# Cross-attention on one core: maxima taken over two heads at a time, masked keys replaced by a mean

## The chip, the core and the metric

The kernel runs on one NeuronCore of a Trainium2 chip. The metric is device time in microseconds: the median of several executions of the whole program, launch to end. A profile is one execution under the hardware profiler, with a time of its own. TensorE does the matrix products, VectorE, ScalarE and GpSimd (POOL in the rows) the elementwise work, and the queue SP issues nearly all DMAs.

## The reference

One cross-attention block in float32: batch B = 4, 512 query tokens, 512 key tokens, width 512, 16 heads of 32, MLP width 2048.

```python
x = layer_norm(hidden_states, ln1_w, ln1_b)
q = x @ q_w + q_b;  k = enc @ k_w + k_b;  v = enc @ v_w + v_b      # split into 16 heads of 32
scores = einsum('bhqd,bhkd->bhqk', q, k) / sqrt(32)
scores = where(mask, scores, finfo.min)                            # mask: (B, keys)
out = einsum('bhqk,bhkd->bhqd', softmax(scores), v) @ cproj_w + cproj_b
hidden = out + hidden_states
y = gelu(layer_norm(hidden, ln2_w, ln2_b) @ fc_w + fc_b) @ proj_w + proj_b
return hidden + y
```

## The kernel before, in words

**Precision.** Every product is made of three float32r matmuls: each operand is split into a high part (its float32r rounding) and a low part (the rest), and high times high, low times high and high times low are summed in PSUM (`mm3`, L487 to L489). So each product tile needs a rounding and a subtraction by ScalarE, VectorE or GpSimd.

**Stage 1, projections** (batch b = 0 to 3). For each batch TensorE computes V (4 units), K (4 units g = 0 to 3) and Q (4 units). Each unit is 12 matmuls. ScalarE writes a unit's high part (`qk_high`, L778), VectorE its low part (`qk_low`, L994), into one of four buffers `QK`; SP stores both to DRAM (`store_qk`, L269). A buffer is written again four units later and waits for both stores. On VectorE the LN1 statistics and norms of the next batch (`x_norm`, L930 to L943) and the affine step (`x_affine`, L986) lie between these. `x_turn(1)` (L547), TensorE's transposes of batch 1, comes after batch 0's last Q unit and before batch 1's V, and waits for all four norms of `x_norm(1)`. GpSimd makes the low parts of weights, context and x (`low`, L1224), in a fixed order.

**Stage 2, attention.** Sets s = 0 to 15: set s holds the four heads j = 0 to 3 of batch s // 4, group s % 4. Softmax needs a maximum per head and query. It is taken over *leading scores*: the product of the high parts alone. `s1(group)` (L579) computes, for one set and one block of 128 queries, the four heads' 128x512 tiles into the four PSUM banks 0 to 3, in one go; `maximum(tile)` (L1007) reads one bank, adds the mask row (0 or a huge negative number, spread over 128 partitions in SBUF by `load_mask`) and takes the maximum into one column of `mx`. There are 64 groups and 256 tiles. Groups 0 to 7 lie between the last batch's projections; the loop of 64 passes `i` (s = i // 4, kc = i % 4) does group 8 + i in pass i, for i up to 55. One ring (`RB`) orders everything that uses banks 0 to 3; `s1` waits until all earlier places are evicted.

In a pass TensorE runs, in program order: the exact transposed scores of key block kc (`s2`, L594, four tiles, three PSUM banks in turn; the mask is a row of the stacked operand), `s1` of the group ahead, P times V of pass i - 2 (`pv`, L610), at kc = 0 the transpose of the maxima (L586), at kc = 2 the sums of the previous set (`sums`, L625), and in some odd passes from i = 17 on (and 56 to 59) a *piece* of the output projection (`cproj`, six matmuls) into a bank of the same ring. `s1` of the next pass stands behind all that. ScalarE takes the exponentials (`exp`, L796). VectorE takes the group's maxima, then the divide steps of an older set (`divide_a`, L1012, at kc = 2 once the sums are there; L1016; L1022 at kc = 0), then adds the piece to the residual (L1134), later the pair adds of probabilities (L1036, which GpSimd does before pass 56, L1324), and for batch 0 the LN2 statistics (passes 36 to 44), the block transposes `y_block` (passes 48, 49, 52, 53) and the affine steps `y_affine` (L962, all four in pass 56). The transposed blocks of LN2 go out to DRAM (`y_store`) and come back (`y_load`, issued at pass 54); `y_affine` waits for their landing. ScalarE and GpSimd then split them (`Y_HIGH`, `Y_LOW`: passes 57 to 59).

**Stage 3, MLP.** 64 passes of `fc` and `pj`, nearly all TensorE.

Each engine executes its own program in order; a wait at the head of a queue holds everything behind it.

## Time and profile before

| | us |
|---|---|
| median of 3 executions | 779.47 (778.07 to 779.97) |
| the profiled execution | 775.62 |
| its span | 773.8 |
| TensorE busy | 745.1 (96%) |
| VectorE busy | 461.9 (60%) |
| ScalarE busy | 281.4 (36%) |
| GpSimd busy | 292.9 (38%) |
| the 256 masked maxima, rows' own time | 169.0 (84.5 + 84.5) |
| chain that ended last: TensorE, VectorE | 77%, 15% of the span |

Busy time counts overlapping rows once. Stage 1 ends and the attention loop begins at about 152 us from the start of the span, the loop ends at about 408 us. In a timeline row the first two numbers are the start and the length in us, then come engine, line, operation, output <- input, the shapes and a count; the bracket gives how long the engine stood idle before it and what released it.

### The profile page before, as it was taken

To read this page: it belongs to the slowest core of one execution; us is meant where nothing else is said; L and a number is where in the kernel's file an instruction comes from. 1 tells how busy PE (TensorE), PEld (TensorE's weight loads), DVE (VectorE), ACT (ScalarE), POOL (GpSimd) and SP (SyncE) were. 2 spreads that over 40 slices of the span, in tenths; PEclk is the share of its full clock that TensorE was granted. 3 is DMA by queue.
4 is the path that set the end of the run, shared out by engine and by line. 5 is a ranking of instruction groups with operands and counts; after the bars stand their busy time and mean duration, and the time that the engine had idled before them with its cause. 6 is when DMAs were issued, how large, how long until landed. Compare 5 with 4: busy or idle time off the path is not lost.

```text
span 773.8 us, 10036 instructions
## 1 busy us (share of the span) xinstructions
PE 745.1 (96%) x3664; PEld 515.3 (67%) x3664; DVE 461.9 (60%) x999; ACT 281.4 (36%) x492; POOL 292.9 (38%) x179
## 2 busy tenths in 40 slices
PE   6999999889899999999989999999999999999998
PEld 5878886633344444444436888888888888888886
DVE  6673346789988888999768578534413343232213
ACT  4434241276766666666763011211112111211110
POOL 2654150067898778799734002122002200230000
PEclk9999999999999999999999999999999999999999
DMA  9656377597656785578640637240220404030001
GB/s 327 227 169 226 126 212 245 186 253 167 171 141 153 189 217 150 156 204 181 173 136 28 191 102 211 82 163 1 42 68 1 163 14 97 1 108 1 1 0 55
DMA packets 94385, 103.25 MB, mean 133 GB/s; under 512 B 39968, under 2 KB 48420, under 8 KB 94336
## 3 DMA queue, kind: packets, MB, share of 16 engines
q1 hardware_dynamic: 94192, 102.59, 46.1%
q8 instruction: 29, 0.48, 0.3%
q14 instruction: 20, 0.16, 0.1%
q10 hardware_dynamic: 144, 0.02, 0.0%
HBM read 73.08 MB, written 29.37 MB: 132 GB/s over the span
## 4 chain that ended last, share of the span: by engine, by line
PE 77%; DVE 15%; DMA 2%; issue 2%; ACT 2%; SPq 1%; POOL 0%; DVEq 0%; ACTq 0%
PE ps L487 21%; PE ps L489 21%; PE ps L488 21%; DVE ps L1007 8%; PE ps L610 4%; PE ps L594 4%; PE ps L579 3%; PE ps L625 2%; DVE R L1134 2%; DMA yt<-FU 1%; DVE mx L1007 1%; PE ps L547 1%; ACT Pt L796 1%; DVE R L943 1%; DVE V L1036 1%
## 5 line engine op out<-in xcount | busy, mean ns | idle before, releaser
L796 ACT ACTIVATE Pt<-ps 128x512 f32<-128x512 f32 x256 | 137.6, 597 | 75.0 <-PE ps L594 74.2
L1181 DVE CAST HR<-R 128x512 fp32r<-128x512 f32 x52 | 25.1, 483 | 184.7 <-ACT R L831 184.7
L831 ACT ACTIVATE R<-ps,cols 128x512 f32<-128x512 f32 x52 | 35.9, 690 | 227.2 <-PE ps L489 227.1
L594 PE MATMUL ps<-BIG 98*128 98x512 f32 x256 | 92.9, 440 | 6.5 <-ACT Pt L796 2.6
L1007 DVE CUSTOM_DVE_ANT_0 ps<-ps,FU 128x512 f32<-128x512 f32 x128 | 84.5, 722 | 14.4 <-PE ps L579 14.2
L594 PEld LDWEIGHTS ps<-BIG 98*128 98x128 f32 x256 | 44.6, 189 | 70.3 <-issue 29.2
L1007 DVE CUSTOM_DVE_ANT_0 ps<-ps,BIG 128x512 f32<-128x512 f32 x128 | 84.5, 723 | 8.4 <-PE ps L579 8.4
L487 PE MATMUL ps<-BIG,HR 128*128 128x512 f32 x192 | 74.8, 390 | 0.7 <-DVE HR L1183 0.7
L487 PE MATMUL ps<-YT,BIG 128*128 128x512 f32 x192 | 74.9, 390 | 0.0
L488 PE MATMUL ps<-YT,BIG 128*128 128x512 f32 x192 | 74.7, 389 | 0.0
L489 PE MATMUL ps<-BIG,HR 128*128 128x512 f32 x192 | 74.7, 389 | 0.0
L489 PE MATMUL ps<-YT,BIG 128*128 128x512 f32 x192 | 74.7, 389 | 0.0
L488 PE MATMUL ps<-BIG,HR 128*128 128x512 f32 x192 | 74.7, 389 | 0.0
L610 PE MATMUL ps<-Pt,V 128*32 128x512 f32 x512 | 68.2, 605 | 0.0
L1324 POOL TENSOR_TENSOR R<-Pt 128x1024 f32<-128x1024 f32 x20 | 47.8, 2409 | 49.0 <-ACT Pt L796 49.0
L487 PE MATMUL ps<-BIG 128*128 128x512 f32 x128 | 53.1, 415 | 5.9 <-DVE BIG L1075 5.9
L1224 POOL TENSOR_TENSOR YT<-R,YT 128x512 fp32r<-128x512 f32 x12 | 15.4, 1308 | 109.1 <-ACT YT L848 109.1
L1324 POOL TENSOR_TENSOR RAWY<-Pt 128x1024 f32<-128x1024 f32 x22 | 52.9, 2426 | 4.0 <-ACT Pt L796 4.0
L1224 POOL TENSOR_TENSOR BIG<-R,BIG 128x512 fp32r<-128x512 f32 (+1 forms) x27 | 36.7, 1377 | 42.6 <-ACT BIG L808 23.0
L488 PE MATMUL ps<-BIG 128*128 128x512 f32 x128 | 51.5, 402 | 0.0
L489 PE MATMUL ps<-BIG 128*128 128x512 f32 x128 | 51.4, 401 | 0.0
L487 PE MATMUL ps<-BIG,WK 128*128 128x512 f32 x128 | 50.8, 397 | 0.0
(133 smaller groups left out, 1375.3 us busy)
## 6 DMA issues: line engine op xcount, KB each, us to landing
BIG<-qs SPq DMA_DIRECT2D x62, 256.0 KB, 2.9
BIG<-ks SPq DMA_DIRECT2D x62, 256.0 KB, 3.2
ks<-BIG SPq DMA_DIRECT2D x32, 256.0 KB, 2.1
qs<-BIG SPq DMA_DIRECT2D x32, 256.0 KB, 5.2
R<-hd SPq DMA_DIRECT2D x28, 256.0 KB, 4.1
R<-in_x SPq DMA_DIRECT2D x16, 256.0 KB, 5.9
hd<-R SPq DMA_DIRECT2D x16, 256.0 KB, 3.9
yt<-FU SPq DMA_DIRECT2D x64, 64.0 KB, 2.1
```

The lines of the kernel that those rows point to most:

```text
L487: eng.matmul(outp, a[0], b[0], start=first, stop=False)
L488: eng.matmul(outp, a[1], b[0], start=False, stop=False)
L489: return eng.matmul(outp, a[0], b[1], start=False, stop=last)
L579: eng.matmul(bank(bank_b(RB[("s1", 4 * group + j)])), lead(s)[r, 0, qc * 128:(qc + 1) * 128], lead(s)[r, 1, :], start=True, stop=True).the ...
L594: eng.matmul(bk, K_[0:98, j, kc * 128:(kc + 1) * 128], Q_[0:98, j, :], start=True, stop=True).then_inc(S["p_ra"], 1)
L610: ins = eng.matmul(bank(7)[32 * j:32 * j + 32, :], V[:, 4 * b + kc, c:c + 32], Pt[:, r, j % 2, :], start=kc == 0, stop=kc == 3)
L796: eng.activation(Pt[:, r, j % 2, :], bank(bank_a(("s2", i, j))), ACT.Exp, scale=SCALE).then_inc(S["a_ra"], 1)
L831: eng.activation(g, bank(4 + i % 2), ACT.Gelu_apprx_tanh, bias=fcb[:, f:f + 1]).then_inc(S["a_g"], 1)
L1007: eng.tensor_tensor_reduce(out=scores, in0=scores, in1=MASK[s // 4], scale=1.0, scalar=-3.4e38, op0=ALU.add, op1=ALU.max, accum_out=mx[:, ...
L1181: eng.tensor_copy(HR[:, n, 0, :], g).then_inc(S["v_hh"], 1)
L1224: eng.tensor_tensor(dst, src, high.bitcast(F32), ALU.subtract).then_inc(S[name], 1)
L1324: eng.tensor_tensor(pair(m)[:, 2 * hp:2 * hp + 2, :], Pt[:, (r - 2) % 6, :, :], Pt[:, r, :, :], ALU.add).then_inc(S["g_ac"], 1)
```

## The change

1. The maxima are no longer taken tile by tile with the mask. `maxima(n)` takes two heads (two PSUM banks, 1024 elements per partition) in one `tensor_reduce` that writes two columns of `mx`: 128 instructions for 256. `s1` signals after every second matmul, and the ring has two places per group for four. The mask rows in SBUF, their four loads and the semaphores go away.
2. So that masked keys can't win a maximum, their columns in the leading part of K are replaced by the mean of the kept keys' columns. `keys(b)` (six small and middle VectorE instructions per batch) makes two rows, `kept` and `share`, from the mask's bytes, which one new DMA spreads over the partitions early; `keep` (a multiply with a running sum, then a multiply-add) rewrites one 128x512 tile. For batches 0 to 2 that is `keep_key`, straight after each K unit's `qk_low`, and the store of the high part waits for it. For batch 3 it is `keep_lead(s)`, on the loaded leading part, in passes 38, 42, 46 and 50. `keys(3)` is in pass 0.
3. The negated maxima get a bias for rows with no kept key, in the same ScalarE instruction.
4. The projection pieces have fixed banks, 0 or 2. A piece waits for the first pair of the current group to be evicted.
5. The `y_affine` steps move from pass 56 to 58, `Y_HIGH` to 59 and 60, `Y_LOW` to 60 and 61.
6. The load of `cbt` moves from stage 1 to pass 2, behind a wait for `keys(3)`'s first step.

```diff
-        MASK = [FU[:, 0, :], FU[:, 1, :], BIG[:, 2048:2560].bitcast(F32), BIG[:, 2560:3072].bitcast(F32)]
+        bits = cbt[:, :].bitcast(U8)
+        def kept(b):
+            return FU[:, 0, :] if b < B - 1 else BF[:, 2048:2560]
+        def share(b):
+            return FU[:, 1, :] if b < B - 1 else BF[:, 2560:3072]
...
-        Y_NORM, Y_BLOCKS, Y_AFFINE = (45, 47, 49, 51), (48, 49, 52, 53), (56, 56, 56, 56)
-        Y_HIGH, Y_LOW = (57, 57, 58, 58), (58, 58, 59, 59)
+        Y_NORM, Y_BLOCKS, Y_AFFINE = (45, 47, 49, 51), (48, 49, 52, 53), (58, 58, 58, 58)
+        Y_HIGH, Y_LOW = (59, 59, 60, 60), (60, 60, 61, 61)
...
-        def bank_b(place):
-            return place % 4
+        def bank_cp(i):
+            return 2 if i in (56, 58) else 0
...
# SP
-                for h, done in ((0, ("a_qh", kq + 1)), ...
+                for h, done in ((0, ("a_qh", kq + 1) if which or b == B - 1 else ("v_kf", 4 * b + g + 1)), ...
-            def load_mask(b):
...
+            eng.dma_start(bits, mask.rearrange("b t -> (b t)").partition_broadcast(128)).then_inc(S["d_bits"], 16)
...
                 if i == 2:
-                    load_mask(1)
-                if i in (12, 28):
-                    load_mask(2 if i == 12 else 3)
+                    sp.wait_ge("v_mc", 4)
+                    eng.dma_start(cbt[:, :], c_b.partition_broadcast(128)).then_inc(S["d_cb"], 16)
...
# TensorE
             def s1(group):
                 s, qc = divmod(group, 4)
                 pe.wait_ge(f"d_hi{s % 2}", 32 * (s // 2 + 1))
-                ring_b(RB[("s1", 4 * group + 3)])
+                if s >= 4 * (B - 1):
+                    pe.wait_ge("v_kf", s + 1)
+                place = RB[("s1", 2 * group)]
+                if place:
+                    pe.wait_ge("v_rb", place)
+                else:
+                    pe.wait_ge("v_fu", 16)
                 for j in range(4):
                     r = slice(32 * j, 32 * j + 32)
-                    eng.matmul(bank(bank_b(...)), lead(s)[r, 0, ...], lead(s)[r, 1, :], start=True, stop=True).then_inc(S["p_rb"], 1)
+                    ins = eng.matmul(bank(j), lead(s)[r, 0, ...], lead(s)[r, 1, :], start=True, stop=True)
+                    if j % 2:
+                        ins.then_inc(S["p_rb"], 1)
...
                 if i in PIECES:
                     n, c, half = PIECES[i]
-                    bk = ring_b(RB[("cp", n, c, half)])
-                    cproj(n, c, (2 * half, 2 * half + 1), bk).then_inc(S["p_rb"], 1)
+                    if i in GROUPS:
+                        pe.wait_ge("v_rb", RB[("s1", 2 * GROUPS[i])] + 1)
+                    else:
+                        pe.wait_ge("v_rb", RB[("cp", n, c, half)] - 1)
+                    cproj(n, c, (2 * half, 2 * half + 1), bank(bank_cp(i))).then_inc(S["p_rb"], 1)
...
# VectorE
-            def maximum(tile):
...
-                eng.tensor_tensor_reduce(out=scores, in0=scores, in1=MASK[s // 4], scale=1.0, scalar=-3.4e38, op0=ALU.add,
-                                         op1=ALU.max, accum_out=mx[:, s % 2, 4 * j + qc:4 * j + qc + 1]).then_inc(S["v_rb"], 1)
+            def keys(b):
+                dve.wait_ge("d_bits", 16)
+                if b == B - 1:
+                    dve.wait_ge("p_pj", 40)
+                eng.tensor_copy(kept(b), bits[:, 512 * b:512 * b + 512]).then_inc(S["v_mc"], 1)
+                dve.wait_ge("v_mc", b + 1)
+                eng.tensor_reduce(out=cnt[:, b:b + 1], in_=kept(b), op=ALU.add, axis=AX.X).then_inc(S["v_ct"], 1)
+                dve.wait_ge("v_ct", b + 1)
+                eng.tensor_scalar(rn[:, b:b + 1], cnt[:, b:b + 1], 1.0, -1.0, ALU.max, ALU.mult).then_inc(S["v_cm"], 1)
+                eng.tensor_scalar(nz[:, b:b + 1], cnt[:, b:b + 1], 0.0, 2.0 ** 127, ALU.is_equal, ALU.mult).then_inc(S["v_nz"], 1)
+                dve.wait_ge("v_cm", b + 1)
+                eng.reciprocal(rn[:, b:b + 1], rn[:, b:b + 1]).then_inc(S["v_rn"], 1)
+                dve.wait_ge("v_rn", b + 1)
+                eng.tensor_scalar(share(b), kept(b), 1.0, rn[:, b:b + 1], ALU.subtract, ALU.mult).then_inc(S["v_sh3"], 1)
+            def keep(s, part):
+                b = s // 4
+                dve.wait_ge("v_sh3", b + 1)
+                eng.tensor_tensor_reduce(out=part, in0=part.bitcast(F32), in1=kept(b), scale=1.0, scalar=0.0, op0=ALU.mult,
+                                         op1=ALU.add, accum_out=ksum[:, s % 4:s % 4 + 1]).then_inc(S["v_ks"], 1)
+                dve.wait_ge("v_ks", s + 1)
+                eng.scalar_tensor_tensor(out=part, in0=share(b), scalar=ksum[:, s % 4:s % 4 + 1], in1=part.bitcast(F32),
+                                         op0=ALU.mult, op1=ALU.add).then_inc(S["v_kf"], 1)
+            def keep_key(b, g):
+                dve.wait_ge("v_ql", 8 * b + g + 1)
+                keep(4 * b + g, QK[(8 * b + g) % 4][:, 0, :])
+            def keep_lead(s):
+                dve.wait_ge(f"d_hi{s % 2}", 32 * (s // 2 + 1))
+                keep(s, lead(s)[:, 1, :])
+            def maxima(n):
+                group, h = divmod(n, 2)
+                s, qc = divmod(group, 4)
+                dve.wait_ge("p_rb", RB[("s1", n)] + 1)
+                if s >= 2:
+                    dve.wait_ge("p_ra", RA[("mt", s - 2)] + 1)
+                eng.tensor_reduce(out=mx[:, s % 2, 8 * h + qc:8 * h + qc + 5:4], in_=ps[h][:, :, :], op=ALU.max,
+                                  axis=AX.X).then_inc(S["v_rb"], 1)
...
+            keys(0)
             dve.wait_ge("d_raw00", 32)
             eng.tensor_copy(WKQ[2][:, 0:2, :], raw[0][:, 0:2, :]).then_inc(S["v_hi"], 1)
             for b in range(B):
...
                 if 0 < b < 3:
                     x_norm(b + 1)
+                    keys(b)
                 for g in range(4):
                     if b == 0 and g == 2:
                         x_affine(0)
                     qk_low(b, g, 0)
+                    if b < 3:
+                        keep_key(b, g)
...
+                if i == 0:
+                    keys(B - 1)
                 if kc == 2 and s >= 1:
                     divide_a(s - 1)
...
+                if kc == 2 and 4 * (B - 1) <= s + 3 < NS:
+                    keep_lead(s + 3)
```

## Rows read from the trace of the kernel before

**Rows 1.** The stretches by engine (us busy of each, granted clock, DMA), three of them.
```profile
60.00:100.00 40.00, 40.00 (x186) 33.35 (x185) 15.23 (x28) 13.40 (x21) 10.80 (x7) 1.00 0.51 184
...
160.00:200.00 40.00, 35.90 (x216) 12.56 (x212) 36.12 (x98) 28.17 (x56) 30.41 (x15) 1.00 0.73 171
...
386.00:393.00 7.00, 4.37 (x18) 2.99 (x11) 4.25 (x5) 3.93 (x9) 7.00 (x5) 0.78 0.34 117
```

**Rows 2.** VectorE's groups, shapes apart: the masked maxima, and a small one.
```profile
L1007 DVE CUSTOM_DVE_ANT_0 ps<-ps,FU 128x512 f32<-128x512 f32 x128 | 84.5, 722 | 14.4 <-PE ps L579 14.2
...
L939 DVE TENSOR_SCALAR ve<-mv 128x4 f32<-128x4 f32 x8 | 1.4, 170 | 0.3
```

**Rows 3.** Timeline of the leading scores on TensorE, passes 13 and 14.
```profile
199.39 0.51 PE L579 MATMUL ps<-BIG 32*128 32x512 f32 x4 [0.35 <-DVE mx L1007]
...
202.68 0.51 PE L579 MATMUL ps<-BIG 32*128 32x512 f32 x4 [0.46 <-DVE mx L1007]
```

**Rows 4.** Timeline of the same, passes 40 to 42, and VectorE at 40.
```profile
308.37 0.51 PE L579 MATMUL ps<-BIG 32*128 32x512 f32 x4 [0.17 <-DVE R L1134]
...
308.87 0.70 DVE L1007 CUSTOM_DVE_ANT_0 ps<-ps,BIG 128x512 f32<-128x512 f32 x1 [0.48 <-PE ps L579]
...
311.62 0.50 PE L579 MATMUL ps<-BIG 32*128 32x512 f32 x4 [0.33 <-DVE mx L1007]
...
315.98 0.51 PE L579 MATMUL ps<-BIG 32*128 32x512 f32 x4
```

**Rows 5.** Timeline of VectorE and TensorE in the first batch's projections.
```profile
21.73 0.68 DVE L1088 CAST WK<-RAWY 128x1024 fp32r<-128x1024 f32 x1
...
26.30 2.96 DVE L986 TENSOR_SCALAR R<-ps,cols 128x512 f32<-128x512 f32 x4
...
33.27 0.39 PE L487 MATMUL ps<-BIG,WK 128*128 128x512 f32 x1
...
33.51 2.46 DVE L930 BATCH_NORM_STATS2 st<-R 128x6 f32<-128x512 f32 x4
...
37.59 6.06 DVE L943 TENSOR_SCALAR R<-R,mv,rs 128x512 f32<-128x512 f32 x4 [1.13 <-POOL rs L1229]
...
43.70 1.97 PE L547 MATMUL ps<-ident,R 128*128 128x128 f32 x16 [0.74 <-DVE R L943]
```

**Rows 6.** Timeline of GpSimd in the same stretch.
```profile
22.49 4.75 POOL L1224 TENSOR_TENSOR WK<-RAWY,WK 128x1024 fp32r<-128x1024 f32 x2 [3.41 <-DVE WK L1088]
...
27.85 5.04 POOL L1224 TENSOR_TENSOR BIG<-R,BIG 128x512 fp32r<-128x512 f32 x4 [0.62 <-ACT BIG L762]
...
37.52 4.92 POOL L1224 TENSOR_TENSOR BIG<-RAWY,BIG 128x1024 fp32r<-128x1024 f32 x2
```

**Rows 7.** Timeline: one subtraction of two SBUF tiles on VectorE, alone and beside GpSimd.
```profile
178.16 0.64 DVE L1145 TENSOR_TENSOR BIG<-R,BIG 128x512 fp32r<-128x512 f32 x1
...
201.82 5.16 POOL L1324 TENSOR_TENSOR R<-Pt 128x1024 f32<-128x1024 f32 x2
...
202.48 2.26 DVE L1145 TENSOR_TENSOR BIG<-R,BIG 128x512 fp32r<-128x512 f32 x1
```

**Rows 8.** Timeline around pass 39: the divide's transpose, TensorE's projection piece, GpSimd.
```profile
303.41 0.72 DVE L1012 STREAM_TRANSPOSE R<-ps 128x512 f32<-128x512 f32 x1 [0.48 <-PE ps L625]
...
305.94 0.39 PE L487 MATMUL ps<-BIG 128*128 128x512 f32 x1
...
306.24 1.30 POOL L1224 TENSOR_TENSOR BIG<-BF,BIG 128x512 fp32r<-128x512 f32 x1 [3.06 <-ACT BIG L808]
```

**Rows 9.** Timeline of passes 57 to 59: the affine step, the transpose, TensorE.
```profile
378.77 2.66 DVE L962 TENSOR_SCALAR HN<-HN,cols 128x512 f32<-128x512 f32 x2 [1.96 <-DMA HN<-yt]
...
381.82 2.32 DVE L962 TENSOR_SCALAR HN<-HN,cols 128x512 f32<-128x512 f32 x2 [0.39 <-DMA HN<-yt]
...
388.52 0.70 DVE L1012 STREAM_TRANSPOSE R<-ps 128x512 f32<-128x512 f32 x1
...
389.27 0.72 PE L594 MATMUL ps<-BIG 98*128 98x512 f32 x2 [2.63 <-DVE R L1012]
```

More of the change, by code:

```diff
@@ L62, in cross_attention_block @@
         mT = sb("mT", [16, 128], R)
+        kk = sb("kk", [128, 16], F32)
+        cnt, rn, nz, ksum = [kk[:, 4 * i:4 * i + 4] for i in range(4)]
         def part(base, off, k):
@@ L180, in plan_rings @@
         def plan_rings():
-            a, b, seats = {("mt", 0): 0}, {("s1", n): n for n in range(4 * EARLY)}, [("mt", 0)]
+            a, b, seats = {("mt", 0): 0}, {("s1", n): n for n in range(2 * EARLY)}, [("mt", 0)]
             for i in range(NI):
@@ L194, in plan_rings @@
                 if i in GROUPS:
-                    for j in range(4):
-                        b[("s1", 4 * GROUPS[i] + j)] = len(b)
+                    for h in range(2):
+                        b[("s1", 2 * GROUPS[i] + h)] = len(b)
                 if i in PIECES:
@@ L266, in store_qk @@
                 scr = (ks, qs)[which]
-                for h, done in ((0, ("a_qh", kq + 1)), (1, ("v_ql", kq + 1) if (b, g, which) != (*LAST_Q, 1) else ("g_ql", 1))):
+                for h, done in ((0, ("a_qh", kq + 1) if which or b == B - 1 else ("v_kf", 4 * b + g + 1)), (1, ("v_ql", kq + 1) if (b, g, which) != (*LAST_Q, 1) else ("g_ql", 1))):
                     sp.wait_ge(*done)
@@ L562, in ring_a @@
                 return bank(bank_a(item))
-            def ring_b(place):
-                if place >= 4:
-                    pe.wait_ge("v_rb", place - 3)
-                else:
-                    pe.wait_ge("v_fu", 13 + place)
-                return bank(bank_b(place))
             def s1(group):
@@ L1090, in _ @@
                 if b == 3:
-                    for j in range(12):
-                        maximum(j)
+                    for n in range(6):
+                        maxima(n)
                 if 0 < b < 3:
                     x_norm(b + 1)
+                    keys(b)
                 for g in range(4):
@@ L1098, in _ @@
                     qk_low(b, g, 0)
+                    if b < 3:
+                        keep_key(b, g)
                     if b == 3 and g in EARLY_K:
-                        for j in range(4):
-                            maximum(4 * EARLY_K[g] + j)
+                        for h in range(2):
+                            maxima(2 * EARLY_K[g] + h)
                 if b == 0:
@@ L1111, in _ @@
                     if b == 3 and g in EARLY_Q:
-                        for j in range(4):
-                            maximum(4 * EARLY_Q[g] + j)
+                        for h in range(2):
+                            maxima(2 * EARLY_Q[g] + h)
             for i in range(NI):
@@ L1119, in _ @@
                 if i in GROUPS:
-                    for m in range(4):
-                        maximum(4 * GROUPS[i] + m)
+                    for h in range(2):
+                        maxima(2 * GROUPS[i] + h)
+                if i == 0:
+                    keys(B - 1)
                 if kc == 2 and s >= 1:
@@ L1133, in _ @@
                         dve.wait_ge("g_xc", 4 * n + c + 1)
-                    eng.tensor_tensor(R2[:, c, :], bank(bank_b(place)), R2[:, c, :], ALU.add).then_inc(S["v_rb"], 1)
+                    eng.tensor_tensor(R2[:, c, :], bank(bank_cp(i)), R2[:, c, :], ALU.add).then_inc(S["v_rb"], 1)
                 if kc == 3 and s >= 1:
```

34 lines of the change are left out of this document (10 added, 24 removed).

## The prediction

> **What bounds the kernel now.** I read the stretches by engine first: they say which engine sets the pace of each stage, which the totals of the whole span can't. In stage 1 TensorE is without a gap (40.00 of 40 us) while VectorE has 25 us to spare; in the attention loop both are nearly full (35.90 and 36.12) [rows 1]. So a VectorE microsecond is worth something only in the loop, and a TensorE stall in stage 1 is lost for good.
>
> Next the masked maxima: 256 of them, a row of 0.722 us each [rows 2], and the question is which passes wait for them. The timeline of `s1` answers it. Early in the loop an `s1` stands idle on VectorE's `mx` (0.35 and 0.46) and passes are 3.29 long [rows 3]: 0.5 of matmuls, then the group's maxima, then the next `s1`. From pass 16 on a block of four passes takes 16.3 us, and in only one of the four does `s1` wait for maxima: in 40 to 41 (3.25 us, idle 0.33). The `s1` of pass 42 shows no wait, and that of 40 waits 0.17 for the residual add L1134, behind the projection piece, not for maxima [rows 4]. So most of the time VectorE loses on maxima is hidden there.
>
> Last, the timeline of two places that the change touches. In batch 0, `x_turn(1)` waits 0.74 us for VectorE's norms L943: here VectorE's order of work bounds TensorE [rows 5]. And around pass 57, `y_affine` blocks VectorE from 376.8 (378.77 less its idle 1.96) to 384.14, so that the transpose L1012 comes at 388.52 and TensorE stands for 2.63 us [rows 9]; in the 7 us around it the granted clock is 0.78, part of the time at 1.2 in place of 2.4 GHz [rows 1].
>
> **The maxima.** Removed: four instructions per group. On VectorE the group takes 2.70 us from the first start to the release (308.87 to 311.57, 0.05 ahead of `s1` at 311.62 [rows 4]). The trace has no `tensor_reduce`. The nearest row is the statistics instruction, which also reads 512 elements per partition and writes little: four in 2.46, so one starts each 0.60 [rows 5]. Of that 0.53 is a rate of one element per cycle as 512-wide rows have it (0.60 less 0.07 fixed), so 1024 elements take about 1.13 start to start and 1.23 as a row; a pair ends after 1.13 + 1.23 = 2.36, 0.3 sooner than now. The bounds: 2.80 if two banks cost as two rows of 0.70 [rows 4] in sequence (0.1 later than now), and 2.27 if the last row's tail overlaps too. I take 2.36, as the statistics row is of the same kind. The Trainium skill (VectorE: DVE Perf Modes, the TRN2 errata section) charges 120 cycles plus one per element for a PSUM source at 0.96 GHz, an estimate of 1.19 us each and 2.38 a pair; this would change each saving by hundredths.
>
> What it is worth, by place. Between the last projections two `s1` wait for maxima in the timeline: 2 x 0.3 = **-0.6**. In passes 1 to 15 ten intervals hang on VectorE; seven give their full 0.3 (2.1), three others 0.8 together, because other work comes up first; `keys(3)` in pass 0 pushes the next maxima by 0.6, of which 0.2 reaches `s1`: **-2.7**. From pass 16 ten blocks give 0.3 each, -3.1, as TensorE's own work then ends at the same time. In four of them VectorE has statistics or a `y_block` (0.6 to 0.7) ahead of the second pass's maxima, and the piece there now waits for a pair (1.2) where it waited for a single tile (0.7): 4 x 0.45 = 1.8 lost. Together **-1.3**.
>
> **keep_lead.** Four times, in passes 38, 42, 46, 50, two instructions of 512 elements. The nearest row is the subtraction L1145, two SBUF inputs, 0.64 alone [rows 7]; with the reading of the accumulator and a wait between, 1.4 for the two. VectorE's queue puts them behind L1012, which in pass 38 ends at 304.13 [rows 8]; GpSimd is idle then, until 306.24. Queued behind them are the maxima of the next pass, which began 0.3 after L1012; they come 1.1 late, and the piece, which started at 305.94 [rows 8], waits for the first pair until 306.85. That pass is one of those bound by the piece and L1134, so 0.9 is lost each time: **+3.6**. It would be nothing if the pass had slack; its idle of 0.17 on L1134 [rows 4] excludes that.
>
> **keys and keep_key, batches 1 and 2.** Three instructions of 0.6 and three of 0.17 [rows 2, 5], 2.3 us per `keys`, and 1.4 to 3.5 per `keep_key`. VectorE's 25 idle us in 40 cover them [rows 1]; without that cover it would be 8 us a batch. The later stores of K delay no buffer, as it is rewritten four units later (11 us). I take 0. The spread of the mask's bytes (256 KB) is out 15 us ahead of its use; the four mask loads that go away hid behind other work: 0.
>
> **keys(0) and keep_key(0, g).** Here the cover is thin, and this is the largest term. I walk VectorE's queue. `keys(0)` stands before L1088, which moves from 21.73 to 23.95 [rows 5]. GpSimd's two lows of q_w, 2.4 each, follow it and move from 22.49 to 24.7 [rows 5, 6]. The question is whether the two-input `keep` instructions are held by GpSimd. The row of before that is of this kind says so: L1145 takes 0.64 alone and 2.26 when GpSimd's pair add is under way, and it ends 0.6 after that pair add does [rows 7]. The four norms do the same: 6.06 for four, two of them waiting out GpSimd's 4.92 [rows 5, 6]. So: `qk_low` 0 ends at 25.3; the first instruction of `keep` waits for GpSimd until 27.1, the second for the other low until 30.1 and ends at 30.75; `qk_low` 1 and an unheld `keep` end at 32.85. `x_affine(0)` starts there instead of at 26.30. GpSimd's four lows of x follow 1.55 behind (27.85 before [rows 6]), so from 34.4; `keep` 2 is held twice and pushes the last low to 40.7; `keep` 3 ends at 42.1. The statistics of batch 1 start at 42.1 instead of 33.51, and the norms and `x_turn(1)` come 8.6 later. TensorE meanwhile waits for the lows of x: Q's first unit, second half, moves from 33.27 [rows 5] to 40.7, so it reaches `x_turn(1)` at 50.4 and still waits until 52.3. Loss **+8.6**. The other bound is the same walk with nothing held: 2.2 for keys, 5.6 for four `keep`, less the idle gaps in between: the statistics start at 36.0, **+2.5**. I take 8.6, by rows 7.
>
> The Trainium skill (SBUF — State Buffer, Who interferes with whom) has the rule: a VectorE instruction with two SBUF inputs contends with a GpSimd instruction that reads SBUF. The trace agrees (0.64 against 2.26); that a multiply with a running sum falls under it no row of before shows. By the rule the term is 8.6, without it 2.5.
>
> **y_affine to pass 58.** VectorE then runs the pair adds of pass 57 at once, L1012 comes at about 383.6 when the sums are there, and TensorE's 2.63 us go, and with them 7.0 x 0.22 = 1.5 of clock: -4.1. The data land at 381.8, before VectorE gets to pass 58 (385.9), so the wait goes and isn't moved. Given back: ScalarE's two-by-two roundings (1.1 each pair) now lie in passes 59 and 60, where exponentials set the pace: +1.0. **-3.1**, bounds -4.1 and 0.
>
> **Sum.** 8.6 - 0.6 - 2.7 - 1.3 + 3.6 - 3.1 = +4.5. Against the profiled execution (775.62) that is 780.1. The median of the runs is 779.47, 3.85 above it, and I forecast what runs will show: 784.0. A measurement of this kernel tells about 0.3% (2.3 us) from no change.
>
> **Rivals.**
> *Slower still: the reduction over two banks is no shorter than two rows* (the fusion doesn't do what it says). Then a group takes 2.80 us, 0.44 more than I take, on some 22 waits, with the piece's wait longer too: +10, 794 at the worst, 790 with the tail gain. For: no row shows a reduce. Against: statistics start each 0.60. Chance 0.10.
> *Nothing is held and the tail gives all.* Place: batch 0, VectorE between 25 and 42. Price: 2.5 for 8.6, and -4.1 for -3.1: the sum is 4.5 - 6.1 - 1.0 = -2.6, **776.9, faster**. It decides from the point where the statistics of batch 1 start before about 36. For: L1007, with one input in PSUM, is not held beside GpSimd (its rows stay 0.70 to 0.73). Against: rows 7. Chance 0.17.
> *Held in part.* Only one of the two instructions of `keep` is held, or GpSimd falls in other gaps: +4 to 5 in batch 0, sum near 0, 779.5. For: the walk above hangs on who comes first by tenths. Chance 0.23.
> *The forecast.* 0.50.
>
> Slower by over 0.3%: forecast and first rival, 0.60; within: the third, 0.23; faster: 0.17. The range takes in the second rival's 776.9 and, above, the forecast with no tail gain (787) and part of the first rival: 777 to 789. The forecast's own range is 781 to 788.
>
> **What would show it.** `tensor_reduce` rows near 1.23, 128 of them, start to start 1.13; `s1` of pass 41 not waiting for VectorE. In batch 0: `keep` rows of 2 us and more beside GpSimd, the statistics of batch 1 at 42, `x_turn(1)` near 52, TensorE idle some 8 us between 32 and 52. The two `keep_lead` rows at 0.65 and pass 39 about 0.9 longer. No stall near pass 58, clock 1.00 there. Wrong, if `keep` rows stay at 0.65 in batch 0, if `x_turn(1)` starts before 47, or if the reduces take 1.4.

## The result, and the profile after

| us | before | after |
|---|---|---|
| median (20 executions each, same chip) | 778.88 | 781.48 |
| fastest, slowest | 772.72, 789.61 | 780.90, 790.94 |
| profiled execution, span | 775.62, 773.8 | 781.28, 779.5 |
| maxima, rows' own time | 169.0 in 256 | 150.6 in 128 |

The ratio after to before is 1.006 (95%: 1.0035 to 1.0086): slower, by less than the 784.0 forecast. The medians hide something: the fastest executions differ by 8.2 us, not by 2.6. 19 of the 20 of after lie between 780.9 and 784.0. Of before, 8 lie between 772.7 and 774.9 and 11 between 778.0 and 782.8. Those are not two clean groups: before was timed again beside the experiments, and there 21 of 94 executions fill the gap between (one of 1844 us is left aside). The experiments come back to this. Their ratios are against the executions of before taken beside each of them (medians 777.1 to 778.5).

The views answer to those of before. First the groups of VectorE's lines, and for the two instructions of `keep` on a K unit the forms with shortest, median and longest row.

```profile
L1044 DVE TENSOR_REDUCE mx<-ps 128x2 f32<-128x1024 f32 x128 | 150.6, 1219 | 22.0 <-PE ps L581 22.0
```

```profile
L1024 DVE CUSTOM_DVE_ANT_0 BIG<-BIG,FU x12: 691/693/2316, 25.4 to 112.1; 128x512 fp32r<-128x512 f32 x12
```

```profile
L1027 DVE SCALAR_TENSOR_TENSOR BIG<-FU,kk,BIG x12: 752/752/2767, 27.8 to 112.9; 128x512 fp32r<-128x512 f32 x12
```

A reduce takes 1.219 us for two tiles, where [rows 2] had 0.722 for each: 0.23 less. The `keep` instructions are 0.69 and 0.75 where nothing is in their way, and up to 2.32 and 2.77. (The 2.77 stands in batch 2, at 112.87, where it costs nothing.) What happens in batch 0, the timeline of VectorE there says (to be read against [rows 5]):

```profile
24.61 0.74 DVE L999 SCALAR_TENSOR_TENSOR BIG<-ps,cols,BIG 128x512 fp32r<-128x512 f32 x1
25.39 2.32 DVE L1024 CUSTOM_DVE_ANT_0 BIG<-BIG,FU 128x512 fp32r<-128x512 f32 x1
...
27.75 2.75 DVE L1027 SCALAR_TENSOR_TENSOR BIG<-FU,kk,BIG 128x512 fp32r<-128x512 f32 x1
...
31.20 0.69 DVE L1024 CUSTOM_DVE_ANT_0 BIG<-BIG,FU 128x512 fp32r<-128x512 f32 x1
...
31.94 0.75 DVE L1027 SCALAR_TENSOR_TENSOR BIG<-FU,kk,BIG 128x512 fp32r<-128x512 f32 x1
32.61 2.96 DVE L991 TENSOR_SCALAR R<-ps,cols 128x512 f32<-128x512 f32 x4
...
37.63 0.81 DVE L1024 CUSTOM_DVE_ANT_0 BIG<-BIG,FU 128x512 fp32r<-128x512 f32 x1
...
38.48 1.65 DVE L1027 SCALAR_TENSOR_TENSOR BIG<-FU,kk,BIG 128x512 fp32r<-128x512 f32 x1
...
42.23 2.47 DVE L938 BATCH_NORM_STATS2 st<-R 128x6 f32<-128x512 f32 x4
```

GpSimd's rows and TensorE's waits in the same stretch:

```profile
24.77 5.18 POOL L1269 TENSOR_TENSOR WK<-RAWY,WK 128x1024 fp32r<-128x1024 f32 x2 [5.37 <-DVE WK L1126]
34.15 5.42 POOL L1269 TENSOR_TENSOR BIG<-R,BIG 128x512 fp32r<-128x512 f32 x4 [4.20 <-ACT BIG L768]
```

```profile
36.91 0.77 PE L490 MATMUL ps<-BIG,WK 128*128 128x512 f32 x1 [3.99 <-POOL BIG L1269]
52.41 0.77 PE L550 MATMUL ps<-ident,R 128*128 128x128 f32 x5 [1.55 <-DVE R L951]
```

The first `keep` waits out GpSimd's two lows of q_w, one with each of its instructions. The chain of delays is that of the forecast: `x_affine(0)` 6.3 later than in [rows 5], GpSimd's lows of x at 34.15, statistics of batch 1 at 42.23 for 33.51, `x_turn(1)` at 52.41 for 43.70. Busy time by stretch, with TensorE's granted clock ahead of the DMA share, shows the clock down behind TensorE's idle 3.99 us, part of the time at 1.2 GHz:

```profile
35.00:40.00 5.00, 3.09 (x7) 2.12 (x8) 3.66 (x5) 4.19 (x6) 4.58 (x4) 0.58 0.01 3
40.00:45.00 5.00, 5.00 (x17) 4.00 (x17) 4.90 (x13) 0.69 (x1) 0.00 (x0) 0.74 0.65 216
```

To place the rest I took the start of each `s1` group from the timelines and subtracted that of the profile before. Group 8 is pass 0, group 24 pass 16, group 63 pass 55; `pv` is its last pair of matmul rows. Positive is later. The kernels of the experiments are in the same table.

| profile of | group 0 | 8 | 22 | 26 | 44 | 63 | last `pv` |
|---|---|---|---|---|---|---|---|
| before, start us | 119.91 | 151.82 | 202.68 | 218.59 | 292.12 | 368.91 | 406.00 |
| after | +8.72 | +8.01 | +5.96 | +5.69 | +4.46 | +8.53 | +5.26 |
| e1 | 0.14 | 0.15 | -0.18 | 9.09 | 9.11 | 9.04 | 5.78 |
| e2 | 3.82 | 3.10 | 2.07 | 9.16 | 7.96 | 11.99 | 8.73 |
| e3 | 0.69 | -0.07 | -2.29 | -2.56 | -3.79 | 0.25 | -3.02 |
| e4 | 1.82 | 4.31 | 3.34 | 3.07 | 1.89 | 4.97 | 1.70 |
| e5 | 0.27 | 0.28 | 0.49 | 0.21 | 0.25 | 0.25 | -2.06 |
| e6 | 1.42 | 0.71 | -0.33 | -0.60 | -1.77 | 0.58 | -2.69 |
| e7 | 1.00 | 0.29 | -1.65 | -1.91 | -3.12 | -2.66 | -5.94 |
| e8 | 9.00 | 8.53 | 7.51 | 13.99 | 13.43 | 18.64 | 15.38 |
| e9 | 0.39 | 0.40 | -0.08 | 4.34 | 4.38 | 4.40 | 2.10 |
| e10 | 0.15 | 0.11 | 1.33 | 6.10 | 6.07 | 6.05 | 4.06 |
| e11 | 9.32 | 8.59 | 7.65 | 7.41 | 6.16 | 10.19 | 7.88 |
| e12 | 3.07 | 3.94 | 2.94 | 2.71 | 1.55 | 2.02 | -1.24 |

So after loses 8.7 us ahead of the first `s1`, all in batch 0, wins back 3 by pass 18 and another 1.2 by pass 36, loses 4.1 from there to pass 55, and wins 3.3 in the tail.

### The profile page after: what moved, and what is told of

It reads as the page before. It is cut to its first block, busy times and chain, and to the rows that moved or that the text cites. A ratio compares the mean times of both kernels' runs of the same rounds, so it can differ in the third digit from the quotient of the medians.

```text
span 779.5 us, 9725 instructions
## 1 busy us (share of the span) xinstructions
PE 749.3 (96%) x3664; PEld 515.8 (66%) x3664; DVE 480.6 (62%) x687; ACT 281.0 (36%) x492; POOL 297.6 (38%) x179
## 4 chain that ended last, share of the span: by engine, by line
PE 77%; DVE 16%; issue 3%; ACT 2%; DMA 1%; SPq 0%; POOL 0%; DVEq 0%; ACTq 0%; POOLq 0%
PE ps L490 21%; PE ps L492 20%; PE ps L491 20%; DVE mx L1044 6%; PE ps L613 5%; PE ps L597 5%; PE ps L581 3%; PE ps L628 3%; DVE R L1177 2%; DVE R L951 1%; ACT Pt L804 1%; DVE BIG L1188 1%; DMA R<-in_k_w 1%; DVE BIG L1024 1%; PE ps L550 1%
## 5 line engine op out<-in xcount | busy, mean ns | idle before, releaser
L1044 DVE TENSOR_REDUCE mx<-ps 128x2 f32<-128x1024 f32 x128 | 150.6, 1219 | 22.0 <-PE ps L581 22.0
L490 PE MATMUL ps<-BIG,WK 128*128 128x512 f32 x128 | 52.2, 408 | 4.0 <-POOL BIG L1269 4.0
L492 PE MATMUL ps<-BIG,WK 128*128 128x512 f32 x128 | 50.9, 397 | 0.0
```

The source lines that it names most:

```text
L490: eng.matmul(outp, a[0], b[0], start=first, stop=False)
L492: return eng.matmul(outp, a[0], b[1], start=False, stop=last)
L1044: eng.tensor_reduce(out=mx[:, s % 2, 8 * h + qc:8 * h + qc + 5:4], in_=ps[h][:, :, :], op=ALU.max, axis=AX.X).then_inc(S["v_rb"], 1)
```

## The experiments

**e1: before with part 5 alone.** What is the tail gain, without the rest?

```diff
-        Y_AFFINE = ..., (56, 56, 56, 56); Y_HIGH, Y_LOW = (57, 57, 58, 58), (58, 58, 59, 59)
+        Y_AFFINE = ..., (58, 58, 58, 58); Y_HIGH, Y_LOW = (59, 59, 60, 60), (60, 60, 61, 61)
```

> The kernel before with part 5 alone: y_affine in pass 58, the roundings behind it in 59 and 60. My theory: VectorE no longer blocks in pass 56, so TensorE's idle 2.6 us near pass 59 and the lower clock behind it go, and about 1 us comes back in passes 59 and 60: 3.1 us less than the kernel before in its profiled execution (775.6), so about 772.5, ratio 0.996. Rival A (the wait only moves to pass 58): no change, and VectorE idle in front of y_affine there. Rival B (the stall also makes the spread of the runs of before, 772 to 782 us): then these runs lie close together, below all or nearly all of those of before.

Measured: 778.36 (772.58 to 781.79), ratio 1.0004 (0.9969 to 1.0039). In the profile the tail does give 3.3 (9.04 to 5.78), but the median and the fastest execution don't show it. Rival B fell as well, since the runs lie as far apart as those of before. And this profile lost 9.3 us between groups 22 and 26, in passes 14 to 17, where the edit changes nothing. VectorE, GpSimd, TensorE and the stretches there, in this order:

```profile
202.31 5.82 DVE L1145 TENSOR_TENSOR BIG<-R,BIG 128x512 fp32r<-128x512 f32 x1
```

```profile
201.65 4.69 POOL L1324 TENSOR_TENSOR R<-Pt 128x1024 f32<-128x1024 f32 x2
```

```profile
210.79 0.80 PE L579 MATMUL ps<-BIG 32*128 32x512 f32 x4 [3.98 <-DVE mx L1007]
```

```profile
205.00:210.00 5.00, 1.82 (x14) 0.43 (x6) 5.00 (x8) 2.32 (x4) 3.52 (x3) 0.90 1.06 226
210.00:215.00 5.00, 4.21 (x16) 1.46 (x16) 4.12 (x14) 0.78 (x2) 0.31 (x1) 0.50 0.20 75
215.00:220.00 5.00, 5.00 (x18) 1.58 (x18) 3.03 (x9) 2.59 (x6) 4.62 (x2) 0.50 0.02 5
220.00:225.00 5.00, 5.00 (x17) 1.72 (x17) 2.95 (x9) 2.46 (x5) 4.03 (x4) 0.50 0.93 243
225.00:230.00 5.00, 4.91 (x30) 2.63 (x33) 2.48 (x6) 2.40 (x5) 2.52 (x2) 0.90 1.06 225
```

The subtraction L1145 is the very row that [rows 7] show at 2.26 us, one pair add long, started 0.66 behind GpSimd's, as here. Here it lasts 5.82 and waits out both pair adds. In the profile of before GpSimd's two rows take 5.16, here 4.69. I read this as VectorE getting in between the two there and not here. TensorE then stands for 4 us and runs for 15 at 1.2 GHz. Neither price was in my sum, since the one profiled execution of before had been spared them.

**e2: after, with batch 0's `keep` made of two reductions with one input each** (what they write is not the mean: the replacement in batch 0 is left out). The count of instructions, their length and the waits stay; only the second SBUF input goes.

```diff
+                if b == 0:
+                    eng.tensor_reduce(out=ksum[...], in_=part.bitcast(F32), op=ALU.add, axis=AX.X).then_inc(S["v_ks"], 1)
+                    dve.wait_ge("v_ks", s + 1)
+                    eng.tensor_reduce(out=ksum[...], in_=part.bitcast(F32), op=ALU.add, axis=AX.X).then_inc(S["v_kf"], 1)
+                    return
                 eng.tensor_tensor_reduce(
```

> The changed kernel, but keep of batch 0 (four times) is two one-input sums of 512 elements in place of the two two-input instructions; the leading part of batch 0 is not rewritten (masked keys of batch 0 keep their values in the maxima). The same number of instructions, waits and elements. Theory (GpSimd holds two-input instructions): the sums stay at 0.69 us beside GpSimd, the statistics of batch 1 start at about 36 us instead of 42, x_turn(1) near 46 instead of 52.4; 781.3 - 6 = 775. Rival (the cost is the added work and its waits, not the hold): nothing moves, 781.

Measured: 778.11 (775.75 to 786.13), ratio 1.0018 (0.9976 to 1.0059). VectorE's timeline:

```profile
25.47 0.69 DVE L1025 TENSOR_REDUCE kk<-BIG 128x1 f32<-128x512 f32 x1
26.19 0.69 DVE L1027 TENSOR_REDUCE kk<-BIG 128x1 f32<-128x512 f32 x1
...
37.34 2.46 DVE L938 BATCH_NORM_STATS2 st<-R 128x6 f32<-128x512 f32 x4
```

Beside the same two GpSimd instructions no row is longer than 0.69. The statistics start at 37.34 for 42.23 and `x_turn(1)` at 47.51 for 52.41: 4.9 of the 8.7 us are the hold, 3.8 the bare queue time (I had bounded that at 2.5). The fastest execution falls by 5.2. This profile again has the long subtraction in pass 13 (6.18 us) and loses 7.1 between groups 22 and 26, so its total says nothing.

**e3: after without `keep_key` in batch 0** (masked keys of batch 0 are then not replaced).

```diff
-                    if b < 3:
+                    if 0 < b < 3:
                         keep_key(b, g)
```

> The changed kernel without keep_key in batch 0 (masked keys of batch 0 keep their values in the maxima); keys(0) stays. Theory: the statistics of batch 1 start near 33.8 again; keys(0) alone still moves GpSimd's lows of q_w and with them the lows of x by 1.6 us, of which x_turn(1)'s old wait of 0.7 hides a part: 0.5 to 1.2 us of the 8.7 stay, so 781.3 - 7.8 = 773.5. Rival (the loss comes from keys(0) or the mask's DMA at the start): 779 or more.

Measured: 774.45 (772.92 to 780.58), ratio 0.9962 (0.9924 to 1.0001). Group 0 is 8.0 earlier than in after, `x_turn(1)` at 44.18, and the fastest execution falls by 8.0. So four `keep_key` in one batch are 8.0 of the loss of 8.7; those of batches 1 and 2 cost nothing (the differences at `x_turn` 1, 2 and 3 are 8.71, 8.72 and 8.72), as forecast.

**e4: batch 0's replacement moved to the loaded leading parts at the end of stage 1**, where batch 3's is, `keys(0)` to batch 2 (the loads of the mask and of these leading parts move with them), and the `keep_lead` of batch 3 ahead of `divide_a`.

```diff
-            keys(0)
...
                 if b == 3:
+                    keep_lead(0)
+                    keep_lead(1)
                     for n in range(6):
                         maxima(n)
...
                     if b == 3 and g in EARLY_K:
                         for h in range(2):
                             maxima(2 * EARLY_K[g] + h)
+                    if b == 3 and g == 1:
+                        keep_lead(2)
...
+                    if b == 3 and g == 0:
+                        keep_lead(3)
                     if b == 3 and g in EARLY_Q:
```

> The changed kernel with the added work moved to idle places: batch 0's leading parts are rewritten after loading like batch 3's (sets 0 and 1 at the end of batch 2, 2 and 3 between the last projections), keys(0) in batch 2, its rows in a free part of RAWY, and keep_lead in passes 38 to 50 ahead of the divide's transpose. Theory: the 8.7 us of batch 0 go, the 3.7 of keep_lead shrink to at most 0.8, nothing new comes on the path: 781.3 - 8.7 - 3.2 = 769.4, ratio to before 0.988 to 0.992. Rival (the added VectorE work costs its length wherever it lies): the sum of it, 16 keeps of 1.45 and 4 keys of 2.2, stays, and the time is above 778.

Measured: 776.27 (774.22 to 780.77), ratio 0.9979 (0.9947 to 1.0011). Batch 0 is cured (`x_turn(1)` at 44.19), but the median is 6.9 us above the 769.4 expected. In the profile, 1.1 are lost at group 0, where VectorE waits for the landing of the leading part, and 4.1 between groups 6 and 9. The four `keep_lead` still cost 2.6 together (0.30, 0.05, 1.32 and 0.93 for their passes), where 0.8 was expected. There `keep_lead(3)` stands at 147.13 ahead of the maxima of group 6, TensorE waits 1.81 for them, and its granted clock is 0.72, 0.84 and 0.76 in the three stretches from 150 to 165. Not all of the 4.1 is the slot's: e6, which has `keep_lead(3)` elsewhere, still loses 0.8 between the same groups. The difference, 3.3 us, is over twice the 1.4 us that the two instructions take.

**e5: before with the subtractions L1145 made one-input copies** (the low part of the output projection's weights is left out).

```diff
-                    eng.tensor_tensor(WC[1][:, n, :], R2[:, n, :], WC[0][:, n, :].bitcast(F32), ALU.subtract)
+                    eng.tensor_copy(WC[1][:, n, :], R2[:, n, :])
```

> The kernel before, with the four subtractions L1145 (low part of the output projection's weights, two SBUF inputs) made one-input copies; the low part is then not a low part. Theory: the spread of the kernel before comes from this instruction. It is held by GpSimd for one pair add in some executions (2.26 us in the profiled one) and for both in others (5.82 us in the profile of e1), and then TensorE stands for 4 us, the granted clock falls to 0.50 for 15 us, and the execution is 9 us longer. So here no row of L1145 is over 0.8 us, the granted clock is 1.00 from 200 to 230, the fastest execution is 2 to 4 us under that of the kernel before (three rows lose 1.1 to 1.6 us each in a stage that VectorE bounds) and the median falls more than the fastest does: 774 against 778.9. Rival: the spread comes from something else, and the median stays 5 to 6 us above the fastest execution.

Measured: 774.13 (772.56 to 782.47), ratio 0.9989 (0.9951 to 1.0027). The expectation fell: the copies are held too.

```profile
173.29 2.48 DVE L1145 CAST BIG<-R 128x512 fp32r<-128x512 f32 x1
...
178.88 0.38 DVE L1145 CAST BIG<-R 128x512 fp32r<-128x512 f32 x1
...
188.41 1.74 DVE L1145 CAST BIG<-R 128x512 fp32r<-128x512 f32 x1
```

A copy that takes 0.38 alone takes 2.48 beside a pair add, so the hold doesn't need two SBUF inputs. The profile of before had shown that already: the norms L943 read one SBUF tile, with a scalar per partition, and four of them take 6.06 us beside GpSimd in [rows 5] and 1.92 away from it:

```profile
55.55 1.92 DVE L943 TENSOR_SCALAR RAWY<-RAWY,mv,rs 128x512 f32<-128x512 f32 x4 [1.12 <-POOL rs L1229]
```

The reductions of e2, one SBUF input as well, were never held. That is how the Trainium skill has it (SBUF — State Buffer, Who interferes with whom): copies and casts from SBUF can take the shared port, a reduction never does. The five executions from 778.9 to 782.5 among the twelve remain. The profile (773.55) has no long row in pass 13 and a granted clock of 1.00. What the profiled execution of before had lost against this one was in the tail, 2.06 us.

**e6: e4 with the replacement put into measured gaps.**

```diff
-                    keep_lead(1)
                     for n in range(6):
                         maxima(n)
+                    keep_lead(1)
...
+                    if b == 3 and g == 3:
+                        keep_lead(3)
...
-                    if b == 3 and g == 0:
-                        keep_lead(3)
...
-                if kc == 2 and 4 * (B - 1) <= s + 3 < NS:
-                    keep_lead(s + 3)
+                if kc == 2 and 4 * (B - 1) <= s + 3 < NS:
+                    lead_sum(s + 3)
+                if kc == 3 and 4 * (B - 1) <= s + 3 < NS:
+                    keep_add(s + 3, lead(s + 3)[:, 1, :])
```

Here `keep_lead(3)` now follows the last K unit's `qk_low`; `lead_sum` is the first instruction of `keep_lead`, `keep_add` the second.

> e4 with the replacement in gaps that e3 and e4 show on VectorE: keep_lead(1) after the maxima of groups 0 to 2, keep_lead(3) after the last K unit's low part (1.97 us idle there) and no longer ahead of the maxima of group 6, and for sets 12 to 15 the running sum ahead of the transpose of the sums (0.81 us idle) and the multiply-add one pass later ahead of the piece (0.61 us idle). Theory: e4's loss of 4.1 us between groups 6 and 9 was keep_lead(3), which made TensorE stand for 1.8 us, with the clock down behind it; and a keep costs only what it exceeds its gap by. Then: 1.2 us at group 0, nothing at groups 6 to 9 and clock 1.00 there, 0.2 us for each of the four of batch 3 instead of 0.92: profile 771 to 772, median under 774, faster than the kernel before by 0.7 % or more. Rival: VectorE's queue is full anyway and the loss moves to the next wait: 775 to 776 as e4.

Measured: 773.53 (771.62 to 776.82), ratio 0.9959 (0.9928 to 0.999): faster than both kernels. Groups 6 to 8 lose nothing now, so `keep_lead(3)` ahead of the maxima was the cause there. The four `keep_lead` cost 0.46 to 0.49 each, halved but not the 0.2 I expected: in their new places they meet GpSimd.

```profile
300.86 1.05 DVE L1036 CUSTOM_DVE_ANT_0 BIG<-BIG,BF 128x512 fp32r<-128x512 f32 x1
```

```profile
305.10 1.33 DVE L1042 SCALAR_TENSOR_TENSOR BIG<-BF,kk,BIG 128x512 fp32r<-128x512 f32 x1
```

In after the two are 0.65 and 0.75. In pass 0 this profile has a granted clock of 0.66 from 155 to 160 and 1.1 us lost; e3, with the same order in pass 0, has 1.00 and nothing lost.

**e7: e3 without `keep_lead` too** (batches 0 and 3 are not replaced).

```diff
-                if kc == 2 and 4 * (B - 1) <= s + 3 < NS:
-                    keep_lead(s + 3)
```

> The kernel after without the replacement of masked keys for batch 0 and batch 3 (e3 without keep_lead as well). Theory: each of the four keep_lead makes its pass about 0.9 us longer: passes 39, 43, 47, 51 fall by 0.86 to 1.06 each, 3.7 us together, and this ends 3.7 us ahead of e3 (774.45, fastest 772.92): 770.8, fastest about 769.2. Rival: the passes have slack of their own and the keep_lead were hidden: as e3.

Measured: 771.03 (770.01 to 775.27), ratio 0.9916 (0.9881 to 0.9952), against 770.8 expected. Passes 39, 43, 47 and 51 are again as long as before (within 0.04), against +0.86, +0.89, +1.06 and +0.86 in after: `keep_lead` is 3.67 us, on the path in full. The passes 37, 41, 49 and 53 stay 0.43 to 0.46 longer, so that loss has another cause (e12).

**e8: after with one reduction per bank**, four for two.

```diff
-                eng.tensor_reduce(out=mx[:, s % 2, 8 * h + qc:8 * h + qc + 5:4], in_=ps[h][:, :, :], op=ALU.max, axis=AX.X)
+                for k in range(2):
+                    eng.tensor_reduce(out=mx[:, s % 2, 8 * h + qc + 4 * k:...], in_=ps[h][:, k, :], op=ALU.max, axis=AX.X)
```

> The kernel after with four reductions of one bank each in place of two over two banks. Theory (a rate per element plus a fixed part per instruction): rows of 0.69 us, one each 0.60, so a group takes 2.5 us for 2.35 and each of some 22 intervals that hang on VectorE gets 0.15 us back: 784 to 785. Rival (the reduction over two banks is no shorter than two rows): as the kernel after, 781.5, with rows of 0.60 or less. Either way the halved number of instructions is worth no more than 4 us here.

Measured: 791.35 (790.84 to 793.23), ratio 1.0183 (1.0136 to 1.0229). The group of VectorE's lines, and the subtraction in pass 13:

```profile
L1045 DVE TENSOR_REDUCE mx<-ps 128x1 f32<-128x512 f32 x256 | 158.7, 682 | 24.4 <-PE ps L581 24.4
```

```profile
210.05 5.97 DVE L1190 TENSOR_TENSOR BIG<-R,BIG 128x512 fp32r<-128x512 f32 x1
```

Four take 2.48 us by the timeline, where two take 2.36. Against after, e8 loses 1.55 us by group 22 and 1.81 from group 26 to 63, together the 3.3 of the expectation. The other 6.75, between groups 22 and 26, are the long subtraction, with TensorE idle for 3.97 and the clock at 0.50 behind it. After at 2.61 us escapes it in its profile. That the 0.1 us per group of maxima decides this is not shown: e2 has the maxima of after, and the long row as well.

**e9: before with L1145 cut from 512 to 4 elements** (low part left out). **e10: before, unchanged, once more.**

```diff
-                    eng.tensor_tensor(WC[1][:, n, :], R2[:, n, :], WC[0][:, n, :].bitcast(F32), ALU.subtract)
+                    eng.tensor_tensor(WC[1][:, n, 0:4], R2[:, n, 0:4], WC[0][:, n, 0:4].bitcast(F32), ALU.subtract)
```

> The kernel before with the four subtractions L1145 cut from 512 to 4 elements a partition (the low part of the output projection's weights is left out but for these). In e5 the one-input copies in their place were held as well (2.48, 1.74 and 1.99 us), so e5 did not take the hold away; this does. Theory: the spread of the kernel before (772.8 to 786.0 in 26 runs, median 4.4 over the fastest) comes mostly from that hold, by one or by two pair adds of GpSimd. Then three rows of 1.8 to 2.3 us become 0.1, the fastest execution is 769 to 771, and the median stands within 2 us of the fastest, 772 or less. Rival: the clock falls at other waits too, and the spread stays as wide: median 4 us or more above the fastest.

> The kernel before once more, unchanged, for a second profile. Theory: either L1145 in pass 13 lasts 5 to 6 us and the granted clock is down behind it (an execution of 779 or more), or it lasts 2.3 us and the clock is 1.00 there (under 777); the stall at pass 58 is there in both (TensorE idle 1 to 2.6 us). Rival: an execution of 779 or more with L1145 at 2.3 us, the clock down elsewhere.

Measured: e9 776.29 (772.47 to 782.94), ratio 0.999 (0.9954 to 1.0026); e10 779.66. VectorE in pass 13 of e9, and then of e10:

```profile
202.40 5.29 DVE L1145 TENSOR_TENSOR BIG<-R,BIG 128x4 fp32r<-128x4 f32 x1
```

```profile
203.81 5.83 DVE L1145 TENSOR_TENSOR BIG<-R,BIG 128x512 fp32r<-128x512 f32 x1
```

The e9 expectation fell: an instruction of 4 elements is held for 5.29 us as one of 512 is for 5.83. What is held is the start; shortening the instruction takes nothing away, so e9 couldn't answer for the spread. e10 bears the theory out: the unchanged kernel at 779.66 has the long row, TensorE idle for 3.98 at 212.31, 0.77 and 0.88 of the clock behind it, and loses 4.8 between groups 22 and 26. It also loses 1.5 in pass 0, with a granted clock of 0.69 from 155 to 160. And in the tail its stall is 1.50 for 2.63, with the clock at 1.00: it is 2.0 better there than the first profile.

**e11: after with part 5 undone** (the reverse of e1's diff).

> The kernel after with Y_AFFINE, Y_HIGH and Y_LOW back at the passes of the kernel before (56; 57, 58; 58, 59). Forecast as in the prediction: the stall near pass 58 returns, 2.6 us of TensorE and with it the clock: 3.1 to 3.3 us longer, 784.6. Rival, from e1 (median 778.4 against 777.2, fastest 772.6 against 773.0) and e5 (clock 1.00 at 385 to 395 and its last pair of `pv` 2.1 ahead of the profile of before): the clock falls behind that stall only in some executions, and without it the move is worth 0.5 to 1.2 us: fastest 782, median 782 to 783.

Measured: 783.41 (781.93 to 789.48), ratio 1.0109 (1.006 to 1.0157). The rival was right (it had the median at 782 to 783). Two of the six executions are at 789.5. The tail of e11, VectorE, TensorE and the stretch:

```profile
388.48 4.13 DVE L967 TENSOR_SCALAR HN<-HN,cols 128x512 f32<-128x512 f32 x4 [1.51 <-DMA HN<-yt]
```

```profile
398.02 0.73 PE L597 MATMUL ps<-BIG 98*128 98x512 f32 x2 [1.22 <-DVE R L1049]
```

```profile
395.00:400.00 5.00, 3.78 (x21) 2.13 (x20) 3.54 (x4) 4.34 (x8) 5.00 (x4) 1.00 0.13 47
```

The stall is 1.22 and the clock stays at 1.00, against 2.63 and 0.66 in [rows 9]'s execution. From group 63 to the last `pv` e11 gains 2.31 on the profile of before and after gains 3.27, so the move is worth 1.0 us, in the fastest executions too (781.93 and 780.90). Up to pass 56 e11 is the kernel after, and still it loses 1.6 in pass 0, with the clock at 0.81 and 0.85 from 160 to 170, where after loses nothing.

**e12: e6 with LN2's steps behind the maxima they delayed.**

```diff
+                if i in (37, 41):
+                    c = 0 if i == 37 else 2
+                    dve.wait_ge(f"d_h{c}", 16)
+                    statistics(HN, 0, 4, c)
+                if i in (49, 53):
+                    y_block(0, Y_BLOCKS.index(i - 1))
                 if i in PIECES:
...
-                    if i == (36, 37, 40, 41)[c]:
+                    if i == (-1, 37, -1, 41)[c]:
...
-                if i in Y_BLOCKS:
+                if i in (49, 53):
                     y_block(0, Y_BLOCKS.index(i))
```

> e6 with the four VectorE steps of LN2 that stood ahead of a second pass's maxima (the statistics of passes 36 and 40, the block transposes of passes 48 and 52) put behind those maxima, ahead of the residual add of passes 37, 41, 49 and 53, where VectorE is idle for 0.63 us. Theory: the 0.45 that the kernel after loses in each of these passes (a piece that waits for a pair of maxima, the pair late by the step ahead of it) goes: 1.8 us less than e6, fastest 769.9, median 771.7. Rival: the residual add, which the next s1 waits for, comes that much later and the pass is as long as before: as e6, 773.5 and fastest 771.6.

Measured: 773.56 (770.20 to 776.35), ratio 0.9929 (0.9893 to 0.9966). VectorE in pass 37:

```profile
298.30 1.22 DVE L1063 TENSOR_REDUCE mx<-ps 128x2 f32<-128x1024 f32 x1
299.43 0.68 DVE L944 BATCH_NORM_STATS2 st<-HN 128x6 f32<-128x512 f32 x1
300.17 0.69 DVE L1213 TENSOR_TENSOR R<-ps,R 128x512 f32<-128x512 f32 x1
```

Passes 37, 41, 49 and 53 are as long as in before (within 0.05). From group 44 to 63 e12 gains 1.88 on e6, as expected (1.8), and so does the fastest execution (770.20 for 771.62, 1.4). The median isn't lower: this profile has the clock at 0.72 from 125 to 130 and at 0.86 and 0.80 from 155 to 165. That the gain beyond e6 went into such falls of the clock is how I read it; the executions that set the median were not profiled.

## Why the prediction was right, and where its sum was off

It was right in sign, cause and size of the largest term. The time was 2.5 us too high, and the sum itself 1.2 too low; the two errors are of different kinds. By its own steps, against the profiled execution of before:

- **keys(0) and keep_key(0, g), +8.6**: +8.72. Shown by e3 (8.0 back) and e2 (4.9 of it the hold). The statistics came at 42.23 (42.1 forecast), `x_turn(1)` at 52.41 (52.3). One link differed: `keep` 2 was held for 0.1 and 0.9 us, not twice, and GpSimd's last low of x ended at 39.6, not 40.7. Nor did TensorE stand idle for some 8 us between 32 and 52: it stood 3.99 for the first lows of x and 1.55 ahead of `x_turn(1)`, and ran part of the rest with the clock down. The lower bound, 2.5 with nothing held, should have been 3.8 (e2). The walk missed TensorE's clock, which cost nothing here only because `x_turn(1)` waited for VectorE anyway (1.55).
- **Early `s1`, -0.6**: -0.71. **Passes 0 to 15, -2.7**: -1.99. The maxima gave what they should; the subtractions took 0.76 back. They last 2.48, 2.59 and 2.61 instead of 2.02, 1.77 and 2.26 (the last is that of [rows 7]); in pass 13 it now starts 0.32 behind the pair add instead of 0.66. That was the failed step of the sum: I gave VectorE's other rows the lengths of before.
- **Passes 16 to 55, -1.3**: -1.16. Ten first passes of a block 0.31 shorter (forecast 0.3); four second passes +0.42 to +0.46 (0.45), pass 45 +0.17, which I had not seen. e12 shows the cause to be the one named, the step ahead of the maxima and the piece's wait for a pair.
- **keep_lead, +3.6**: +3.67, shown by e7.
- **The reduce, 2.36 a group**: 2.34 to 2.36. The first rival (a fusion that saves nothing) is out, and its 790 was a slip: the 794 held the tail gain already; e8 puts the fusion's own worth at 3.4 us of path, plus what it happens to avoid in pass 13.
- **Tail, -3.1**: -2.9 in the span's end, against that one execution. But 2.0 to 2.3 of it was that execution's bad luck: e5, e9, e10 and e11 all have `Y_AFFINE` at 56 and are that much better there. The move itself is worth 1.0 (e11). The step that failed was "VectorE then ... TensorE's 2.63 us go, and with them ... 1.5 of clock": the stall is 1.22, 1.22, 1.50 and 1.22 in those four and the clock stays up. The transpose that ends the stall stands in VectorE's queue behind the `y_affine` steps, and these ended at 384.14 in the profile of before and at 382.86 in e5's.
- **Sum +4.5, +5.66 measured; then +3.85 "I forecast what runs will show"**: this added the distance between profile and median of before to the kernel after. It doesn't carry over. Of the five profiles of before and of its close relatives (e1, e5, e9, e10), the three at 777 us or more have the long subtraction with the clock down behind it, 4.4 to 9.3 us between groups 22 and 26, and the other two have neither. In after's profile one pair add holds it, and 19 of its 20 executions lie within 3.1 us. So it seems that before pays this price in many of its executions and after in few, which turns a loss of 8.2 us between the fastest into 2.6 between the medians. It is not the only price: pass 0 took 1.5 in e10, and the tail 2.0 to 2.3 in the first profile of before. Nor is after free of it: e11, the same kernel up to pass 56, has two of six executions 6 us above the others, and e2 has the long row.

That 784.0 came within 2.5 us is in part luck. The tail gain was taken 2.1 too large, which made the sum too low, and carrying the sum to the median made it too high by more.

For the executions that were not profiled the place of the loss is argued, not shown. Only their mean granted clock is on record, and it points the same way: beside e1, e5, e9 and e12 the 22 executions of before under 774.5 us have 0.999 or 1.000, the 31 from 780 on have 0.984 to 0.996. What decides between one pair add and two stays open. The start within GpSimd's row does not decide it: 0.66 behind it gave 2.26 and 5.82, 0.3 behind it 2.61 (after) and 6.18 (e2). The clean test, a subtraction away from any pair add, was not tried.

## What to carry to other kernels

Before work is put into VectorE's idle time, look at what GpSimd does then: a step of two instructions with SBUF operands, 1.4 us alone, took 5 beside GpSimd's tensor operations, and in a chain that TensorE waits for all of that is lost, with clock on top. Put such steps into gaps that the timeline shows ahead of a wait (e6, e12), one instruction to a gap. And before a sum is scaled to a median, compare fastest executions and profiles of both: a median can hold the price of an accident that the change happens to avoid.
